# Edge messages of a graph layer on one core: ten routed groups in 28 in place of three in 8, and slot sums after seven of ten routed groups

## The chip, the cores and the metric

The kernel runs on one core of one Trainium2 chip. The metric is device time in microseconds (us): three runs of the kernel before took 2140.23, 2142.25 and 2141.35 us, median 2141.35. The profile is of one more execution, which took 2145.47 us.

## The reference, in short

There are 6250 nodes of 128 numbers and 200,000 edges. Each edge has a source index, a destination index (the edges are sorted by destination), 20 edge features and a weight. All is computed in float32:

```
h    = x @ W_in2f                                      # per node
Wij  = (ssp(f_ij @ W_filt1 + b_filt1) @ W_filt2 + b_filt2) * weight     # per edge
x_ij = h[dst] * Wij                                    # message of an edge
agg  = segment_sum(x_ij, src)                          # added up by source: random order
out  = layernorm(x + ssp(agg @ W_out1 + b_out1) @ W_out2 + b_out2)
```

ssp(v) is softplus(v) - log 2. The gather by destination is over a narrow range of nodes, since the edges are sorted by it. The sum by source is over random nodes, and it is what the change is about.

## The kernel before

**Groups.** Edges are handled in 391 groups of 512 (4 tiles of 128 edges). For each group TensorE computes the filter (first_layer for a pair of groups, second_layer for one), gathers h of the destinations with a one-hot matmul (gather; VectorE's compare_dst makes the one-hot `pick`), ScalarE does the softplus in three passes for each pair (soften_abs, soften_exp, soften_ln) and weighs the gathered rows (weigh_h_dst), VectorE finishes the hidden layer (finish_hidden) and multiplies the message (multiply).

**Two ways to sum by source.** A *plain* group goes to memory: VectorE compares sources (compare_src), TensorE adds up repeated ones inside each tile (sum_repeated), ScalarE copies the totals out of PSUM (copy_total), VectorE makes the indices (mark_repeated, make_index), and GpSimd issues four indirect DMAs that add rows to four tables in HBM (scatter, L778). GpSimd does this for the plain groups in order of their numbers. A *routed* group stays on the chip: ScalarE and VectorE split the message in two parts (split_hi, split_lo), VectorE makes one-hot rows of 896 slots for each of the four tiles (route_one_hot, L1368), TensorE multiplies seven slot tiles of four matmuls each (route, L1726) into unit_psum, and ScalarE copies each tile to a ring in SBUF (keep_slots, L955). A *step* then sums one slot tile number over the newest routed groups: VectorE makes a one-hot of 448 nodes for each (slot_one_hot, L1382, seven buffers), TensorE multiplies (sum_slots, L1746, four matmuls) into unit_psum, and VectorE adds two slices to the accumulator (add_slice, L1397). So each routed group has seven slot tiles to be summed, however many steps there are; a step takes all tiles of its number that lie in the ring.

**Which groups are routed.** Of each period of 8 groups, numbers 1, 4 and 6; after the 48 periods, groups 385 and 388. STEPS_AT says after which routed groups of a period a step is made: after each of the three. TensorE's unit_psum is shared by route and sum_slots, so a step ends only when VectorE has added its slices and the next route begins only when its half is free.

**Order.** Each engine works its instructions in the order in which they are written. For the main stretch this order is written out by hand for one period, in a function `unit(u)` of each engine, and for what is left over in `rest()`. `run_periods` calls unit for every period, unrolled. Every instruction waits on semaphores for what it needs and for its buffer: four buffers each for totals, indices, destination and source loads, two for the one-hot `pick`, and one for route_hot and for moving. SP loads features, dst and src rows and windows in its own written order.

**Last layers.** When all additions have landed, SP loads the four tables (it waits first for the scatter-adds at L710, then for the last slot sum at L711), GpSimd adds them up, and thirteen chunks go through the output layers. The functions that the change touches and their callers follow.

Of the kernel before, what the change touches and what calls it, by code (L numbers as in the profile page):

```python
# [297 lines left out]
def build(nc, t):  # L298
    with ExitStack() as ctx:
# [245 lines left out]
        def _(sp):  # L545
# [114 lines left out]
            def unit(u):  # L660
                def g(n): return plus(u, n)
                def quad(n): return (u[0], u[1] // QUAD + n)
                next_window(g(6))
                next_src(g(7), plain)
                next_dst(g(8))
                next_window(g(7))
                next_dst(g(9))
                next_window(g(8))
                next_src(g(8), plain)
                next_features(quad(6))  # L670
                next_dst(g(10)); next_dst(g(11))
                next_window(g(9)); next_window(g(10))
                next_dst(g(12)); next_dst(g(13))
                next_src(g(10), plain)
                next_window(g(11)); next_window(g(12))
                next_src(g(11), plain)
                next_dst(g(14))
                next_features(quad(7))
                next_src(g(13), plain)
                next_window(g(13))  # L680
                next_dst(g(15))

            def rest():
                next_src((0, 390), plain)
                next_window((0, 390))
# [141 lines left out]
        def _(act):  # L827
# [129 lines left out]
            def unit(u):  # L957
                def g(n): return plus(u, n)
                def pair(n): return (u[0], u[1] // 2 + n)
                def r(n): return (u[0], u[1] // PERIOD * len(ROUTED_AT) + n)  # L960
                copy_total(g(-1), plain)
                soften_abs(pair(2))
                weigh_h_dst(g(2), plain)
                keep_slots(r(-1), 0)
                soften_exp(pair(2))
                copy_total(g(0), plain)
                keep_slots(r(-1), 1); keep_slots(r(-1), 2)
                soften_ln(pair(2))
                keep_slots(r(-1), 3); keep_slots(r(-1), 4); keep_slots(r(-1), 5); keep_slots(r(-1), 6)
                split_hi(r(0))  # L970
                copy_total(g(2), plain)
                weigh_h_dst(g(3), plain)
                soften_abs(pair(3))
                weigh_h_dst(g(4), plain)
                soften_exp(pair(3))
                keep_slots(r(0), 0); keep_slots(r(0), 1)
                soften_ln(pair(3))
                weigh_h_dst(g(5), plain)
                keep_slots(r(0), 2); keep_slots(r(0), 3)
                copy_total(g(3), plain)  # L980
                keep_slots(r(0), 4)
                weigh_h_dst(g(6), plain)
                keep_slots(r(0), 5); keep_slots(r(0), 6)
                soften_abs(pair(4))
                split_hi(r(1))
                soften_exp(pair(4))
                soften_ln(pair(4))
                weigh_h_dst(g(7), plain)
                keep_slots(r(1), 0)
                copy_total(g(5), plain)  # L990
                keep_slots(r(1), 1); keep_slots(r(1), 2)
                weigh_h_dst(g(8), plain)
                soften_abs(pair(5))
                keep_slots(r(1), 3); keep_slots(r(1), 4)
                soften_exp(pair(5))
                soften_ln(pair(5))
                keep_slots(r(1), 5); keep_slots(r(1), 6)
                weigh_h_dst(g(9), plain)
                split_hi(r(2))

            def rest():
                weigh_h_dst((0, 386), plain)
                soften_abs((0, 194))
                keep_slots((0, 143), 0)
                copy_total((0, 383), plain)
                keep_slots((0, 143), 1)
                soften_exp((0, 194))
                keep_slots((0, 143), 2)
                soften_ln((0, 194))
                keep_slots((0, 143), 3)  # L1010
                weigh_h_dst((0, 387), plain)
                keep_slots((0, 143), 4)
                copy_total((0, 384), plain)
                keep_slots((0, 143), 5); keep_slots((0, 143), 6)
                split_hi((0, 144))
                weigh_h_dst((0, 388), plain)
                soften_abs((0, 195))
                soften_exp((0, 195))
                soften_ln((0, 195))
                keep_slots((0, 144), 0)  # L1020
                weigh_h_dst((0, 389), plain)
                keep_slots((0, 144), 1)
                copy_total((0, 386), plain)
                keep_slots((0, 144), 2); keep_slots((0, 144), 3)
                weigh_h_dst((0, 390), plain)
                keep_slots((0, 144), 4)
                copy_total((0, 387), plain)
                keep_slots((0, 144), 5); keep_slots((0, 144), 6)
                split_hi((0, 145))
                keep_slots((0, 145), 0); keep_slots((0, 145), 1)  # L1030
                copy_total((0, 389), plain)
                keep_slots((0, 145), 2); keep_slots((0, 145), 3); keep_slots((0, 145), 4)
                keep_slots((0, 145), 5); keep_slots((0, 145), 6)
                copy_total((0, 390), plain)
# [78 lines left out]
        def _(dve):  # L1113
# [285 lines left out]
            def unit(u):  # L1399
# [13 lines left out]
                slot_one_hot(s(-1), 1)  # L1413
                multiply(g(1), plain)
                slot_one_hot(s(-1), 2)
                compare_src(g(3), plain)
                compare_dst(g(4))
                slot_one_hot(s(-1), 3)
                compare_dst(g(5))
                mark_repeated(g(0), plain)  # L1420
                multiply(g(2), plain)
                slot_one_hot(s(-1), 4)
                make_index(g(0), plain)
                finish_hidden(pair(2))
                slot_one_hot(s(-1), 5)
                route_one_hot(r(0), 0); route_one_hot(r(0), 1)
                slot_one_hot(s(-1), 6)
                route_one_hot(r(0), 2); route_one_hot(r(0), 3)
                split_lo(r(0))
                mark_repeated(g(2), plain)  # L1430
                add_slice(s(-1), 0); add_slice(s(-1), 1)
                make_index(g(2), plain)
                multiply(g(3), plain)
                compare_dst(g(6))
                slot_one_hot(s(0), 0); slot_one_hot(s(0), 1)
                compare_dst(g(7))
                slot_one_hot(s(0), 2); slot_one_hot(s(0), 3)
                multiply(g(4), plain)
                finish_hidden(pair(3))
                slot_one_hot(s(0), 4)  # L1440
                compare_src(g(5), plain)
                compare_dst(g(8))
                slot_one_hot(s(0), 5)
                route_one_hot(r(1), 0); route_one_hot(r(1), 1)
                mark_repeated(g(3), plain)
                slot_one_hot(s(0), 6)
                route_one_hot(r(1), 2)
                slot_one_hot(s(1), 0)
                make_index(g(3), plain)
                multiply(g(5), plain)  # L1450
                slot_one_hot(s(1), 1)
# [493 lines left out]
```

## Time and profile before

| what | value |
|---|---|
| median of three runs | 2141.35 us |
| profiled execution | 2145.47 us |
| its span (first to last instruction) | 2143.7 us |
| TensorE matmul, busy | 2013.4 us |
| VectorE, busy | 1967.4 us |
| ScalarE, busy | 1588.1 us |
| GpSimd, busy | 1664.0 us |
| indirect DMAs of GpSimd | 979 |

Busy time is time in which an instruction of the engine is recorded as running. What lies between two instructions of an engine is idle time, and the profile names what ended it, or says "issue" where it finds nothing that the engine waited for. PE is TensorE, PEld its weight loads, DVE VectorE, ACT ScalarE, POOL GpSimd, and SPq the queue on which SP issues DMAs.

### The profile page before, as it was taken

To read this page: it belongs to the slowest core of one execution; us is meant where nothing else is said; L and a number is where in the kernel's file an instruction comes from. 1 tells how busy PE (TensorE), PEld (TensorE's weight loads), DVE (VectorE), ACT (ScalarE), POOL (GpSimd) and SP (SyncE) were. 2 spreads that over 40 slices of the span, in tenths; PEclk is the share of its full clock that TensorE was granted. 3 is DMA by queue.
4 is the path that set the end of the run, shared out by engine and by line. 5 is a ranking of instruction groups with operands and counts; after the bars stand their busy time and mean duration, and the time that the engine had idled before them with its cause. 6 is when DMAs were issued, how large, how long until landed. Compare 5 with 4: busy or idle time off the path is not lost.

```text
span 2143.7 us, 53463 instructions
## 1 busy us (share of the span) xinstructions
PE 2013.4 (94%) x16433; PEld 1700.4 (79%) x16433; DVE 1967.4 (92%) x4035; ACT 1588.1 (74%) x3852; POOL 1664.0 (78%) x1038
## 2 busy tenths in 40 slices
PE   2589999999999999999999999999999999999946
PEld 2468888888888888888888888888888888888833
DVE  5669999999999999999999999999999999999837
ACT  0278878778788787787877877877878878778517
POOL 2058888888888888888888888888888888888854
PEclk8689999999999999999999999999999999999979
DMA  9546666656666666566666666665666666665574
GB/s 319 212 92 105 102 94 99 104 92 98 102 103 97 100 99 102 90 99 103 95 98 101 100 94 101 99 102 90 99 103 99 96 104 99 102 92 82 89 196 136
DMA packets 346341, 235.28 MB, mean 110 GB/s; under 512 B 86088, under 2 KB 325555, under 8 KB 345851
## 3 DMA queue, kind: packets, MB, share of 16 engines
q0 software_dynamic: 140976, 64.22, 32.6%
q1 hardware_dynamic: 194598, 150.79, 26.9%
q10 hardware_dynamic: 10476, 16.77, 2.1%
q8 instruction: 136, 2.23, 0.4%
q14 instruction: 155, 1.26, 0.2%
HBM read 145.44 MB, written 86.20 MB: 108 GB/s over the span
## 4 chain that ended last, share of the span: by engine, by line
PE 70%; DMA 10%; DVE 8%; issue 6%; POOL 3%; ACT 2%; ACTq 0%; SPq 0%; DVEq 0%; POOLq 0%
PE unit_psum L1726 19%; PE unit_psum L1746 17%; PE both_psum L1682 13%; PE total_psum L1695 8%; DMA table<-total,index 7%; PE pre_psum L1663 7%; PE both_psum L1707 4%; POOL table L778 3%; PE both_psum L1678 2%; DMA src_b<-src 1%; DVE route_hot L1368 1%; DVE scat_hot L1382 1%; DMA b_o<-in_b_o 1%; DVE acc_t L1397 1%; ACT out_rows L1077 1%
## 5 line engine op out<-in xcount | busy, mean ns | idle before, releaser
L778 POOL DMA_INDIRECT table<-total,index x979 | 1605.4, 1640 | 416.6 <-issue 263.9
L1726 PE MATMUL unit_psum<-moving,route_hot 128*128 128x258 f32 x4088 | 637.4, 295 | 2.8 <-DVE acc_t L1397 1.5
L1726 PEld LDWEIGHTS unit_psum<-moving,route_hot 128*128 128x128 f32 x4088 | 526.3, 190 | 48.7 <-ACT ring L955 32.5
L1382 DVE TENSOR_SCALAR scat_hot<-node_iota,ring 128x448 fp32r<-128x448 uint16 x1022 | 473.1, 475 | 17.8 <-PE unit_psum L1746 13.0
L955 ACT ACTIVATE ring<-unit_psum 128x258 fp32r<-128x258 f32 x1022 | 370.3, 402 | 153.0 <-PE unit_psum L1726 139.0
L933 ACT ACTIVATE h_dst<-both_psum,edge_cols 128x128 f32<-128x128 f32 x1564 | 446.1, 379 | 48.8 <-PE both_psum L1707 48.4
L1746 PE MATMUL unit_psum<-scat_hot,ring 64*128 64x448 f32 x4088 | 461.3, 372 | 11.5 <-DVE acc_t L1397 9.7
L1746 PEld LDWEIGHTS unit_psum<-scat_hot,ring 64*128 64x128 f32 x4088 | 378.4, 186 | 87.6 <-ACT ring L955 37.0
L1682 PE MATMUL both_psum<-w_f,hidden 128*128 128x128 f32 x3128 | 422.1, 278 | 0.0
L1368 DVE TENSOR_SCALAR route_hot<-node_iota,slot_cols 128x896 fp32r<-128x896 uint16 x584 | 406.0, 729 | 7.6 <-PE unit_psum L1726 7.0
L1682 PEld LDWEIGHTS both_psum<-w_f,hidden 128*128 128x128 f32 x3128 | 398.5, 192 | 5.5
L896 ACT ACTIVATE soft<-pre_psum 128x1024 f32<-128x1024 f32 x196 | 202.8, 1034 | 101.6 <-PE pre_psum L1663 101.5
L1695 PE MATMUL total_psum<-message,same 128*128 128x129 f32 x1960 | 264.1, 277 | 1.4 <-DVE message L1332 1.4
L1695 PEld LDWEIGHTS total_psum<-message,same 128*128 128x128 f32 x1960 | 240.1, 191 | 4.0 <-DVE message L1332 2.0
L1306 DVE SCALAR_TENSOR_TENSOR hidden<-pre_psum,soft 128x1024 f32<-128x1024 f32 x196 | 237.4, 1211 | 5.6 <-ACT soft L908 5.6
L1663 PE MATMUL pre_psum<-f_t,w_f 32*128 32x512 f32 x784 | 222.8, 644 | 9.0 <-issue 4.0
L915 ACT ACTIVATE total<-total_psum 128x516 f32<-128x516 f32 x245 | 148.7, 607 | 92.7 <-DMA table<-total,index 75.9
L908 ACT ACTIVATE soft<-soft 128x1024 f32<-128x1024 f32 x196 | 212.2, 1083 | 3.1
L902 ACT ACTIVATE soft<-soft 128x1024 f32<-128x1024 f32 x196 | 210.3, 1073 | 0.1
L1397 DVE TENSOR_TENSOR acc_t<-acc_t,unit_psum 128x448 f32<-128x448 f32 x304 | 178.0, 613 | 19.9 <-PE unit_psum L1746 19.1
L1332 DVE TENSOR_TENSOR message<-both_psum,h_dst 128x512 f32<-128x512 f32 x245 | 168.0, 686 | 18.2 <-PE both_psum L1682 14.0
L1707 PEld LDWEIGHTS both_psum<-window,pick 128*128 128x128 bf16 x1564 | 88.7, 98 | 106.5 <-issue 94.3
(124 smaller groups left out, 1561.9 us busy)
## 6 DMA issues: line engine op xcount, KB each, us to landing
dst_b<-dst SPq DMA_DIRECT2D x391, 128.0 KB
src_b<-src SPq DMA_DIRECT2D x245, 128.0 KB
f_t<-in_f_t SPq DMA_DIRECT2D x98, 256.0 KB, 4.1
table<-total,index POOLq DMA_INDIRECT x979
table<-zeros ACTq DMA_DIRECT2D x20, 640.0 KB, 9.9
window<-h_parts SPq DMA_DIRECT2D x391, 32.0 KB
parts<-table SPq DMA_DIRECT2D x48, 256.0 KB, 5.3
h_parts<-h_out SPq DMA_DIRECT2D x12, 384.0 KB, 2.8
```

The source lines that it names most:

```text
L778: pool.indirect_dma_start(tables[k], bass.IndirectOffsetOnAxis(index[:, i, k:k + 1], 0), total[:, i, k, 0:DIM], None, compute_op=ALU.add). ...
L908: act.activation(soft[:, :, :], soft[:, :, :], ACT.Ln, bias=1.0).then_inc(soft_done, 1)
L933: last = act.activation(h_dst[:, b, d], source, ACT.Copy, scale=columns_of(g, kind)[:, weight:weight + 1])
L955: act.activation(ring[:, RING_AT[r[1], k], :], unit_psum[:, k % 2, 0:MOVING], ACT.Copy).then_inc(ring_done, 1)
L1306: dve.scalar_tensor_tensor(hidden[:, first:first + 2, :], pre_psum[:, :, :], 0.0, soft[:, :, :], ALU.max, ALU.add).then_inc(hidden_done, 1)
L1368: hot = dve.tensor_scalar(route_hot[:, tile, :], node_iota[:, :], slot_cols[:, column:column + 1], None, ALU.is_equal)
L1382: dve.tensor_scalar(scat_hot[:, (n - 1) % HOTS, :], node_iota[:, 0:BUCKET], ring[:, RING_AT[r[1], slot_tile(s)], 2 * DIM:2 * DIM + 1].bitc ...
L1663: last = pe.matmul(pre_psum[:, a, :], w_f1[row:row + BAND, :], f_t[row:row + BAND, quad[1] % FEEDS, :], start=True, stop=True)
L1682: last = pe.matmul(filter_psum[:, d], hidden[:, g[1] % QUAD, k * P:(k + 1) * P], w_f2[:, :], start=False, stop=(k == TILES - 1))
L1695: last = pe.matmul(total_psum[:, k // 2, d], same[:, b, k, :], message[:, b, k, :], start=True, stop=True)
L1726: last = pe.matmul(unit_psum[:, k % 2, 0:MOVING], route_hot[:, tile, k * P:(k + 1) * P], moving[:, tile, :], start=(tile == 0), stop=(tile ...
L1746: last = pe.matmul(unit_psum[:, strip, 0:BUCKET], ring[rows, RING_AT[r[1], slot_tile(s)], part * DIM:(part + 1) * DIM], scat_hot[rows, (n ...
```

## The change

The constants of the period change, and with them every written order: SP's, ScalarE's, VectorE's and TensorE's unit and rest. GpSimd's code is the same. No instruction changes its form. The ring, whose size is computed from the constants, has 43 tiles in place of 28.

```diff
-PERIOD = 8
-ROUTED_AT = (1, 4, 6)
-LAST_PERIOD = 384
-LAST_ROUTED = (385, 388)
+PERIOD = 28
+ROUTED_AT = (2, 4, 7, 10, 13, 16, 18, 21, 24, 27)
+LAST_PERIOD = 364
+LAST_ROUTED = (366, 368, 371, 374, 377, 380, 382, 385)
...
-STEPS_AT = (0, 1, 2)
+STEPS_AT = (0, 2, 3, 5, 6, 8, 9)
...
@@ VectorE, unit(u): the first lines of 77 instructions before and of 258 after
-                slot_one_hot(s(-2), 6)
+                route_one_hot(r(-1), 0)
+                slot_one_hot(s(-2), 7)
+                route_one_hot(r(-1), 1)
                 multiply(g(0), plain)
-                split_lo(r(-1))
-                route_one_hot(r(-1), 2); route_one_hot(r(-1), 3)
+                slot_one_hot(s(-2), 8); slot_one_hot(s(-2), 9)
+                route_one_hot(r(-1), 2)
+                mark_repeated(g(-2), plain)
                 slot_one_hot(s(-1), 0)
                 add_slice(s(-2), 0)
-                mark_repeated(g(-1), plain)
-                make_index(g(-1), plain)
+                route_one_hot(r(-1), 3)
+                split_lo(r(-1))
                 add_slice(s(-2), 1)
...
@@ TensorE, unit(u): the first lines
-                sum_slots(s(-2), 1); sum_slots(s(-2), 2); sum_slots(s(-2), 3); sum_slots(s(-2), 4)
-                sum_slots(s(-2), 5); sum_slots(s(-2), 6)
+                route(r(-2), 6)
+                gather(g(2))
+                sum_slots(s(-2), 0); sum_slots(s(-2), 1); sum_slots(s(-2), 2); sum_slots(s(-2), 3)
+                sum_slots(s(-2), 4); sum_slots(s(-2), 5); sum_slots(s(-2), 6); sum_slots(s(-2), 7)
+                sum_slots(s(-2), 8); sum_slots(s(-2), 9)
                 first_layer(pair(2))
-                gather(g(2))
+                gather(g(3))
                 second_layer(g(1))
                 route(r(-1), 0)
...
@@ TensorE, rest(): the end
-                sum_repeated((0, 390), plain)
-                route((0, 145), 5); route((0, 145), 6)
-                sum_slots((0, 145), 0); sum_slots((0, 145), 1); sum_slots((0, 145), 2); sum_slots((0, 145), 3)
...
-                sum_slots((0, 149), 2); sum_slots((0, 150), 0); sum_slots((0, 150), 1); sum_slots((0, 151), 0)
+                sum_repeated((0, 390), plain)
+                sum_slots((0, 100), 0); sum_slots((0, 100), 1); sum_slots((0, 100), 2); sum_slots((0, 100), 3)
+                sum_slots((0, 101), 0); sum_slots((0, 101), 1); sum_slots((0, 102), 0)
```

## Rows read from the trace of the kernel before

**Rows 1.** The page: busy us of each engine, share of the span, instructions.
```profile
PE 2013.4 (94%) x16433; PEld 1700.4 (79%) x16433; DVE 1967.4 (92%) x4035; ACT 1588.1 (74%) x3852; POOL 1664.0 (78%) x1038
```

**Rows 2.** GpSimd in time order, 710 to 752: start us, us, instruction, idle before.
```profile
710.91 1.84 POOL L778 DMA_INDIRECT table<-total,index  x1 [0.30 <-issue]
...
724.53 1.96 POOL L778 DMA_INDIRECT table<-total,index  x1 [0.31 <-issue]
...
742.63 1.54 POOL L778 DMA_INDIRECT table<-total,index  x1 [0.74 <-issue]
744.47 1.54 POOL L778 DMA_INDIRECT table<-total,index  x1 [0.30 <-issue]
746.32 1.54 POOL L778 DMA_INDIRECT table<-total,index  x1 [0.30 <-issue]
```

**Rows 3.** Groups of instructions: busy us, mean ns, idle us before, releasers.
```profile
L778 POOL DMA_INDIRECT table<-total,index x979 | 1605.4, 1640 | 416.6 <-issue 263.9 <-DVE index L1351 107.2 <-DMA table<-total,index 41.3
```

**Rows 4.** VectorE in time order, 710 to 730, columns as in rows 2 (xN: N merged).
```profile
711.03 0.44 DVE L1382 TENSOR_SCALAR scat_hot<-node_iota,ring 128x448 fp32r<-128x448 uint16 x1
711.39 1.27 DVE L1368 TENSOR_SCALAR route_hot<-node_iota,slot_cols 128x896 fp32r<-128x896 uint16 x2
...
725.73 0.67 DVE L1368 TENSOR_SCALAR route_hot<-node_iota,slot_cols 128x896 fp32r<-128x896 uint16 x1
```

**Rows 5.** Single tiles: ns min/median/max, first and last start us.
```profile
L1382 DVE TENSOR_SCALAR scat_hot<-node_iota,ring x1022: 431/444/781, 140.1 to 2046.7; 128x448 fp32r<-128x448 uint16 x171
L1368 DVE TENSOR_SCALAR route_hot<-node_iota,slot_cols x584: 666/679/1024, 129.1 to 2019.8; 128x896 fp32r<-128x896 uint16 x195
L1296 DVE TENSOR_SCALAR pick<-dst_b,edge_cols x391: 333/345/683, 108.3 to 2012.7; 128x512 bf16<-128x512 uint16 x196
L1342 DVE TENSOR_SCALAR moved<-total,order_twice,spare_row x245: 270/279/606, 126.6 to 2031.3; 128x4 f32<-128x4 f32 x123
L1286 DVE TENSOR_TENSOR same<-src_b,edge_cols x245: 671/679/695, 113.7 to 2013.2; 128x512 f32<-128x512 uint16 x123
L1397 DVE TENSOR_TENSOR acc_t<-acc_t,unit_psum x304: 600/614/624, 142.9 to 2055.8; 128x448 f32<-128x448 f32 x152
```

**Rows 6.** Stretches: us, then busy us of PE, PEld, DVE, ACT, POOL, clock, DMA.
```profile
128.90:2046.50 1917.60, 1903.58 (x15909) 1624.45 (x15909) 1840.25 (x3744) 1510.20 (x3687) 1605.40 (x979) 1.00 0.62 99
2046.50:2143.70 97.20, 53.16 (x242) 30.83 (x238) 52.56 (x160) 47.77 (x114) 46.64 (x39) 0.82 0.62 167
```

**Rows 7.** Groups as in rows 3: TensorE's matmuls of the two kinds.
```profile
L1726 PE MATMUL unit_psum<-moving,route_hot 128*128 128x258 f32 x4088 | 637.4, 295 | 2.8 <-DVE acc_t L1397 1.5 <-ACT ring L955 0.3
L1746 PE MATMUL unit_psum<-scat_hot,ring 64*128 64x448 f32 x4088 | 461.3, 372 | 11.5 <-DVE acc_t L1397 9.7 <-ACT ring L955 0.9 <-DVE scat_hot L1382 0.9
L1695 PE MATMUL total_psum<-message,same 128*128 128x129 f32 x1960 | 264.1, 277 | 1.4 <-DVE message L1332 1.4
```

**Rows 8.** Groups as in rows 3: VectorE and ScalarE.
```profile
L1382 DVE TENSOR_SCALAR scat_hot<-node_iota,ring 128x448 fp32r<-128x448 uint16 x1022 | 473.1, 475 | 17.8 <-PE unit_psum L1746 13.0 <-ACT ring L955 2.3
L1397 DVE TENSOR_TENSOR acc_t<-acc_t,unit_psum 128x448 f32<-128x448 f32 x304 | 178.0, 613 | 19.9 <-PE unit_psum L1746 19.1
L1368 DVE TENSOR_SCALAR route_hot<-node_iota,slot_cols 128x896 fp32r<-128x896 uint16 x584 | 406.0, 729 | 7.6 <-PE unit_psum L1726 7.0
L955 ACT ACTIVATE ring<-unit_psum 128x258 fp32r<-128x258 f32 x1022 | 370.3, 402 | 153.0 <-PE unit_psum L1726 139.0
```

**Rows 9.** What SP's queue waited for: us in total, times, longest.
```profile
SPq L623 <- PE both_psum L1707: 513.4, 161, 6.3
SPq L590 <- DVE pick L1296: 479.2, 236, 8.1
...
SPq L711 <- PE unit_psum L1746: 7.1, 1, 7.1
```

**Rows 10.** TensorE in time order, 2048 to 2060.
```profile
2050.97 1.86 PE L1746 MATMUL unit_psum<-scat_hot,ring 64*128 64x448 f32 x8 [1.24 <-DVE acc_t L1397]
2054.08 1.11 PE L1746 MATMUL unit_psum<-scat_hot,ring 64*128 64x448 f32 x4 [1.25 <-DVE acc_t L1397]
```

More of the change, by code:

```diff
@@ L1431, in unit @@
+                mark_repeated(g(1), plain)
+                make_index(g(1), plain)
+                slot_one_hot(s(-1), 9)
+                compare_src(g(5), plain)
                 add_slice(s(-1), 0); add_slice(s(-1), 1)
[L1432 to L1435, printed above, removed]
+                slot_one_hot(s(0), 0)
+                multiply(g(4), plain)
+                slot_one_hot(s(0), 1); slot_one_hot(s(0), 2)
@@ L1462, in unit @@
+                route_one_hot(r(2), 1); route_one_hot(r(2), 2)
+                split_lo(r(2))
+                route_one_hot(r(2), 3)
+                slot_one_hot(s(1), 2)
+                multiply(g(9), plain)
+                slot_one_hot(s(1), 3)
+                mark_repeated(g(6), plain)
+                compare_dst(g(12))
+                make_index(g(6), plain)
+                finish_hidden(pair(6))
+                multiply(g(10), plain)
+                compare_src(g(11), plain)
                 slot_one_hot(s(1), 4)
-                make_index(g(5), plain)
@@ new lines, in unit @@
+                slot_one_hot(s(2), 6)
+                mark_repeated(g(11), plain)
+                slot_one_hot(s(2), 7); slot_one_hot(s(2), 8)
+                finish_hidden(pair(8))
+                slot_one_hot(s(2), 9)
+                compare_dst(g(17))
+                multiply(g(14), plain)
+                split_lo(r(4))
+                make_index(g(11), plain)
+                add_slice(s(2), 0); add_slice(s(2), 1)
+                compare_src(g(15), plain)
+                multiply(g(15), plain)
@@ new lines, in unit @@
+                compare_dst(g(25))
+                slot_one_hot(s(4), 5); slot_one_hot(s(4), 6)
+                route_one_hot(r(7), 0)
+                multiply(g(23), plain)
+                mark_repeated(g(19), plain)
+                split_lo(r(7))
+                compare_dst(g(26))
+                route_one_hot(r(7), 1)
+                make_index(g(19), plain)
+                compare_src(g(25), plain)
+                route_one_hot(r(7), 2)
+                slot_one_hot(s(4), 7)
+                multiply(g(24), plain)
@@ new lines, in unit @@
+                compare_dst(g(28))
+                mark_repeated(g(22), plain)
+                make_index(g(22), plain)
+                route_one_hot(r(8), 0); route_one_hot(r(8), 1); route_one_hot(r(8), 2)
+                split_lo(r(8))
+                route_one_hot(r(8), 3)
+                multiply(g(26), plain)
+                finish_hidden(pair(14))
+                mark_repeated(g(23), plain)
+                compare_dst(g(29))
+                compare_src(g(29), plain)
+                slot_one_hot(s(5), 2); slot_one_hot(s(5), 3)
@@ new lines, in unit @@
+                route(r(4), 1); route(r(4), 2)
+                second_layer(g(16))
+                route(r(4), 3); route(r(4), 4)
+                gather(g(17))
+                route(r(4), 5); route(r(4), 6)
+                sum_repeated(g(14), plain)
+                first_layer(pair(10))
+                gather(g(18))
+                second_layer(g(17))
+                sum_repeated(g(15), plain)
+                route(r(5), 0); route(r(5), 1)
+                second_layer(g(18))
+                route(r(5), 2); route(r(5), 3)
@@ new lines, in unit @@
+                first_layer(pair(12))
+                gather(g(22))
+                route(r(6), 0); route(r(6), 1)
+                second_layer(g(21))
+                route(r(6), 2)
+                sum_repeated(g(19), plain)
+                route(r(6), 3)
+                second_layer(g(22))
+                route(r(6), 4)
+                gather(g(23))
+                route(r(6), 5); route(r(6), 6)
+                first_layer(pair(13))
+                gather(g(24))
+                second_layer(g(23))
```

1103 lines of the change are left out of this document (907 added, 196 removed).

## Prediction

> **What bounds the kernel now.** I read the page's busy shares first. They point at TensorE (94%) and VectorE (92%), and show GpSimd at 78% [rows 1]. The next view is GpSimd's own instructions in time order over one period of eight groups [rows 2]. Each scatter-add starts 0.30 us after the previous one ended, whatever that one took; the reader is to see that the column "idle before" hardly ever rises above 0.30 and is put down to "issue". The shortest scatter-adds last 1.54 us, so the floor of one is 1.54 + 0.30 = 1.844 us from start to start (742.63 to 744.47 to 746.32 shows it). The grouped row [rows 3] gives the whole: 979 of them, mean 1.640 us, 416.6 us idle before them, of which 104.5 us lie before the first. That is 1605.4 + 312.1 = 1917.5 us, from 128.9 to 2046.5 us, which is the whole main stretch. GpSimd is never without work there. It is 78% "busy" and 100% occupied, because the 0.30 us between two scatter-adds is not counted. So the main stretch is 979 x 1.959 us, and of the 1.959 us, 1.844 is floor and 0.115 is waiting.
>
> What is the 0.115? The smaller part is a gap now and then (the 0.74 us before 742.63). The larger, 0.098 us each, is scatter-adds that last longer than 1.54 us. Their long forms stand where VectorE runs one-hot comparisons: the scatter-add at 710.91 took 1.84 us and the one at 724.53 took 1.96 us, while VectorE ran route_hot from 711.39 to 712.66 and from 725.73 [rows 2, 4]. The comparisons are slowed in return: all four kinds of tensor_scalar have a long tail (route_hot 666 to 1024 ns, scat_hot 431 to 781, pick 333 to 683, moved 270 to 606), and the tensor_tensor kinds have none (same 671 to 695, acc_t 600 to 624) [rows 5]. Two parties that stretch each other, and only in one kind of instruction, share something.
>
> TensorE is close behind: 1903.6 us busy of the 1917.6 [rows 6]. VectorE has 1840.3.
>
> **The change, part by part.** Counted from the constants: before there are 48 periods x 3 + 2 = 146 routed and 245 plain groups; after, 13 x 10 + 8 = 138 routed and 253 plain. Steps of slot sums fall from 152 to 103, each taking ten groups' slots instead of seven in the steady part; slot tiles fall from 1022 to 966.
>
> *TensorE.* A routed group costs (637.4 + 461.3) / 146 = 7.53 us in the route and slot-sum matmuls, a plain one 264.1 / 245 = 1.08 us [rows 7]. Eight groups moved: 8 x (7.53 - 1.08) = -51.6 us.
>
> *VectorE.* 56 scat_hot at 0.463 (-25.9), 32 route_hot at 0.695 (-22.2), 8 split_lo at 0.68, the length of the tensor_tensor `same` of equal size [rows 5] (-5.4), 98 slice adds at 0.586 (-57.4); plus 8 x (0.68 + 0.28) = +7.7 for compare_src and mark. Sum -103 us [rows 5, 8]. *ScalarE:* 56 ring copies at 0.362, -20 us [rows 8]; the copies of totals and of moving nearly cancel.
>
> None of these three is worth anything by itself while GpSimd sets the pace: 1903.6 - 51.6 = 1852 us of TensorE lies below even the floor of GpSimd after the change.
>
> *GpSimd.* 8 plain groups more are 32 scatter-adds more, 1011. At the pitch of before this costs 32 x 1.959 = +62.7 us. The floor rises from 1805 to 1011 x 1.844 = 1864.3 us. This is the term that no cover hides.
>
> *The waits of the scatter-adds* are the unknown. Nothing in the trace shows the new orders, so I bound them. Upper end: 0.115 us each, as now: 1980.5 us. Lower end: none at all: 1864.3 us. What is between them: the comparisons' time for each scatter-add, by medians of [rows 5], is now (1022 x 0.444 + 584 x 0.679 + 391 x 0.345 + 245 x 0.279) / 979 = 1.076 us and becomes (966, 552, 391 and 253 of the same) / 1011 = 0.998 us, 7% less. The orders themselves can be counted too: a comparison in a run takes its median less the 0.08 by which neighbours overlap (711.03 to 711.39 for one of 0.44 us [rows 4]), so 0.36 for scat_hot, 0.60 for route_hot, 0.26 for pick and 0.20 for moved. The time by which runs of comparisons, with no other instruction between them, exceed 0.95 us is then 7.4 us in the old unit, 0.37 for each of its 20 scatter-adds, and 18.3 us in the new one, 0.25 for each of 72: ten of twelve route_one_hot stand in pairs before, about half of forty afterwards. (The 0.95 is half of the floor of 1.844, an estimate of what fits once the scatter-add must get in twice; it serves to compare the orders and no more.) Scaled with the first the stretch of 0.098 becomes 0.091, with the second 0.067. I take the second and 0.010 for gaps, 0.077 in all, because VectorE also gets a real reserve (103 us) in which its comparisons can be late without anyone waiting. Pitch 1.921, stretch 1942.1 us.
>
> The Trainium skill (SBUF - State Buffer, "Who interferes with whom") says that a VectorE instruction in a 2-port mode and a GpSimd instruction exclude each other for the whole length, and that tensor_scalar may enter that mode where tensor_tensor may not. The second half agrees with the tails above. The first half does not hold here as it stands: 1.076 us of comparisons and 1.54 us of scatter-add cannot lie one behind the other in 1.959 us.
>
> *Queues.* SP issues 8 more src loads of 128 KB and places all its loads in the new order; it waits for VectorE and TensorE for nearly 1000 us of the span in the two longest entries [rows 9], so its loads are early. Cost 0, or 1 us per load that comes late. The scatter's order on GpSimd is unchanged: group by group.
>
> *Start.* The first scatter-add waits for the first total; group 0 is plain in both. The routing tables of 584 columns shrink to 552 ahead of it: -1.5 to 0, taken as 0. It stays at 128.9.
>
> *End.* Now the last landed scatter-add is not the last event: SP's wait on the tables ends, and then it waits 7.1 us more for the last slot sum [rows 9], because after the last total TensorE still has 28 slot tiles in seven short steps, each handed over by VectorE's adds (1.24 and 1.25 us idle before the last two [rows 10]). After the change only 7 tiles in 3 steps stand behind the last sum_repeated, while the last five groups (386 to 390) are all plain and give GpSimd 19 scatter-adds in a row. So GpSimd ends last and the 7.1 us go: the tail of 97.2 us [rows 6] becomes 90.1. Bounds 97.2 and 90.1; what is late next is GpSimd itself.
>
> *Sum.* 128.9 + 1942.1 + 90.1 = 2161 us of span, against 128.9 + 1917.6 + 97.2 = 2143.7. The profiled execution took 2145.5, 1.8 above its span, and the median of the runs is 2141.35, 4.1 below that. So take 2.3 off: **2159 us**, 0.8% slower. With bounds of the wait: 2081 (none) to 2197 (as now). Equality is at a pitch of (2143.7 - 219.0) / 1011 = 1.904 us, a wait of 0.060 us: the change gains only if it halves what the scatter-adds wait.
>
> **Rivals.**
>
> *A. The waits do not fall.* Comparisons still meet a scatter-add as often as they do now. 0.095 to 0.115 us each gives 2179 to 2197. For it: the comparisons' time falls by 7% only, and a phase between two engines over 72 scatter-adds is harder to hold than over 20. Against: VectorE's reserve.
>
> *B. Faster: each microsecond of comparison that is taken away gives its whole length back.* Place: the main stretch. Price: 1.076 - 0.998 = 0.078 us for each scatter-add, so the wait falls to 0.037 and the pitch to 1.881: 1901.7 + 219.0 = 2121, **2118 us**. It decides from a wait of 0.060 down. For it: TensorE is 99% busy now, so GpSimd's waits of before may have been in the shadow of a TensorE that had no more to give, and with 52 us less there they are free to shrink; three large ones of a period (0.30 and 0.42 of length, and the gap's 0.44 above 0.30 [rows 2]) are 1.2 of its 20 x 0.115 = 2.3 us, and an order that avoids those alone stands at 0.055. Against: the many small ones remain. (The Trainium skill's lock for the whole length, in the section named above, is the reading by which all the time taken away comes back.)
>
> *C. The engines are bound by TensorE as before and GpSimd keeps up.* Then the 51.6 us of TensorE would show in full: 2141 - 52 = 2090. Against: GpSimd's floor alone gives 2081, and it would need waits of 0.009. I give it the low end of B only.
>
> *D. A new wait.* A step sums ten slot tiles, and there are seven scat_hot buffers, so TensorE can hold unit_psum half way while VectorE writes three more; the route matmuls and ring copies queue behind. 1 us in each of 103 steps, if GpSimd runs dry by it: 2159 + 50 at most. Against: TensorE has some 90 us of reserve below 1942.
>
> **How the numbers follow.** Two runs of this kernel can be told apart from about 0.2%, 4.3 us, a wait of 0.004 us up or down: "the same" is a wait of 0.056 to 0.064. Chances: forecast (0.064 to 0.095) 0.34; A 0.17; D 0.03; the same 0.08; B with C 0.38. So faster 0.38, same 0.08, slower 0.54. The range leaves out the waits under 0.03 and over 0.114: 2112 to 2196. The likeliest case by itself is 2146 to 2178.
>
> **What would show it.** GpSimd: 1011 scatter-adds, gaps of 0.30 throughout, mean length near 1.60 us; under A 1.63 and more, under B 1.57. The first at 128.9 and the last near 2069. TensorE less busy in the main stretch than its 99% now, VectorE near 90%. SP's wait for the slot sum gone. If GpSimd's idle time in front of scatter-adds grows beyond 0.32 us each with "DVE index" or "ACT total" as releaser, the bound has moved and the argument is wrong; if the mean length is below 1.58 us, only the size of the wait was.

## The result, and the profile after

The changed kernel takes **2227.26 us** (median of four runs, 2219.77 to 2230.95) against 2141.52 us for the kernel before beside it. The ratio is 1.0398, 95% interval 1.0377 to 1.0418: 4% slower. The forecast of 2159 us had the direction right; the size was wrong, and the time lies above the range of 2112 to 2196.

The page of the changed kernel, busy us of each engine, with the granted clock in 40 slices. It answers to [rows 1].

```profile
PE 2018.5 (91%) x16049; PEld 1677.4 (76%) x16049; DVE 1879.1 (85%) x3865; ACT 1575.2 (71%) x3788; POOL 1721.6 (78%) x1070
...
PEclk8589999999999999999999999999999999999969
...
L860 POOL DMA_INDIRECT table<-total,index x1011 | 1663.0, 1645 | 443.8 <-issue 278.7
```

The shares of PE and DVE fell and GpSimd's stayed at 78%. The last line answers to [rows 3]: 1011 scatter-adds as counted, mean 1.645 us (1.640 before). The two stretches that answer to [rows 6], then three short ones; columns as there (us, busy us of PE, PEld, DVE, ACT, POOL, clock, DMA share, GB/s):

```profile
127.30:2129.30 2002.00, 1911.44 (x15547) 1603.45 (x15545) 1756.36 (x3580) 1495.17 (x3617) 1662.97 (x1011) 0.98 0.61 96
2129.30:2217.80 88.50, 47.92 (x212) 27.93 (x212) 47.89 (x150) 47.72 (x114) 46.66 (x39) 0.83 0.70 183
427.80:434.60 6.80, 6.80 (x30) 5.07 (x30) 4.62 (x10) 3.78 (x11) 5.89 (x4) 0.50 0.43 52
571.20:578.00 6.80, 6.60 (x27) 4.87 (x28) 5.28 (x11) 3.69 (x11) 5.69 (x4) 0.50 0.49 59
578.00:694.00 116.00, 111.44 (x925) 93.70 (x924) 103.44 (x212) 89.92 (x216) 95.12 (x59) 1.00 0.59 93
```

The main stretch is 2002.0 us, 1011 x 1.980. The two short stretches show something that the main stretch of before did not have until its last few steps: TensorE at a granted clock of 0.50, that is 1.2 GHz, while it is busy. Read through in consecutive stretches of a few us, there are twelve such places up to 2107 us, five of some 6.8 us and seven of some 3.4, 58 us in all. In the kernel before there is none between 125 and 2033 us.

The terms of the prediction's own sum, in us. The floor is 1.54 us of scatter-add and 0.304 us to the next one:

| term | predicted | measured | before |
|---|---|---|---|
| start, to the first scatter-add | 128.9 | 127.3 | 128.9 |
| floor, 1.844 each | 1864.3 | 1864.3 | 1805.3 |
| scatter-adds longer than 1.54 | 67.7 | 106.1 | 97.7 |
| gaps above 0.304 | 10.1 | 31.7 | 14.6 |
| tail | 90.1 | 88.5 | 97.2 |
| span | 2161.1 | 2217.8 | 2143.7 |
| median less span | -2.1 | +9.5 | -2.3 |

(Measured: 1663.0 - 1011 x 1.54 = 106.1, and 2002.0 - 1663.0 - 1011 x 0.304 = 31.7.) Two terms failed, both inside "the waits of the scatter-adds": 60 us of the miss of 68. These waits, the stretch and the gaps together, are 0.136 us each, not 0.077. Start and tail take 3 back, and the other runs of the changed kernel lie 6 to 11 us above the profiled one, so that its median is 9.5 above the span.

**Where the gaps come from.** Before, [rows 2], the idle time in front of a scatter-add was 0.30 us almost always. GpSimd of the changed kernel, in time order:

```profile
595.84 2.09 POOL L860 DMA_INDIRECT table<-total,index  x1 [0.30 <-issue]
599.38 1.55 POOL L860 DMA_INDIRECT table<-total,index  x1 [1.45 <-issue]
...
605.41 1.59 POOL L860 DMA_INDIRECT table<-total,index  x1 [0.30 <-issue]
609.37 1.91 POOL L860 DMA_INDIRECT table<-total,index  x1 [2.37 <-issue]
```

The profile says "issue", but VectorE made the index of the scatter-add at 599.38 only at 598.37:

```profile
597.77 0.68 DVE L1571 TENSOR_TENSOR same<-src_b,edge_cols 128x512 f32<-128x512 uint16 x1
598.37 0.15 DVE L1636 TENSOR_TENSOR index<-moved,edge_cols 128x4 int32<-128x4 f32 x1
```

GpSimd runs dry there. Of such gaps 20 are over 0.6 us; from 462 us on they come one to three times in each period of some 143 us. Ahead of them, ScalarE and TensorE in time order:

```profile
566.40 0.40 ACT L1037 ACTIVATE ring<-unit_psum 128x258 fp32r<-128x258 f32 x1
570.47 0.60 ACT L997 ACTIVATE total<-total_psum 128x516 f32<-128x516 f32 x1 [3.67 <-DMA table<-total,index]
570.97 0.66 ACT L1037 ACTIVATE ring<-unit_psum 128x258 fp32r<-128x258 f32 x2
```

```profile
566.48 1.22 PE L2306 MATMUL unit_psum<-moving,route_hot 128*128 128x258 f32 x8
567.54 0.40 PE L2287 MATMUL both_psum<-window,pick 128*128 128x128 bf16 x4
571.40 2.09 PE L2306 MATMUL unit_psum<-moving,route_hot 128*128 128x258 f32 x8 [3.46 <-ACT ring L1037]
```

ScalarE's copy of the totals (L997) waits 3.67 us until the scatter-adds that read the same one of the four buffers have landed. The ring copy stands behind it in ScalarE's order, and the route matmuls wait for the ring copy, so TensorE idles 3.46 us. After that the same eight matmuls take 2.09 us in place of 1.22: the clock has been halved. A second way leads over VectorE. At 691.46 the copy of the totals waited 4.04 us; VectorE's mark of repeated rows waits for that copy, a comparison stands behind the mark, and TensorE waits for the comparison:

```profile
692.09 0.29 DVE L1627 TENSOR_SCALAR moved<-total,order_twice,spare_row 128x4 f32<-128x4 f32 x1 [2.61 <-ACT total L997]
692.50 0.67 DVE L1667 TENSOR_SCALAR scat_hot<-node_iota,ring 128x448 fp32r<-128x448 uint16 x1
693.22 0.67 PE L2326 MATMUL unit_psum<-scat_hot,ring 64*128 64x448 f32 x4 [2.77 <-DVE scat_hot L1667]
```

ScalarE's waits for landings, in all, times, and longest, of the changed kernel and of before:

```profile
ACT total L997 <- DMA table<-total,index: 140.4, 56, 11.6
```

```profile
ACT total L915 <- DMA table<-total,index: 75.9, 62, 3.3
```

Of the 140.4, 17.7 lie in two waits of the last plain groups (2098.82 and 2108.62); the others above 2.5 us come about once a period or twice, as at 385, 530, 675, 816 and 960, and at 427, 570 and 691. Of the 20 large gaps of GpSimd 16 follow an idle time of TensorE of 1.98 us or more, by 26 to 56 us. A fall of the clock is not needed for it: one of 0.93 us at 1175.6 follows an idle time of 2.11, and one of 2.18 at 1475.3 an idle time of 2.77, and after both the granted clock stayed at 1.00:

```profile
1141.92 1.22 PE L2306 MATMUL unit_psum<-moving,route_hot 128*128 128x258 f32 x8 [2.11 <-ACT ring L1037]
...
1428.84 1.22 PE L2306 MATMUL unit_psum<-moving,route_hot 128*128 128x258 f32 x8 [2.77 <-ACT ring L1037]
```

That the idle times bring the gaps about is read from this order of events; experiment 4 tests it.

### The profile page after: what moved, and what is told of

It is laid out like the page before. It is cut to its first block and busy times, and to the rows that moved or that the text cites. A ratio compares the mean times of both kernels' runs of the same rounds, so it can differ in the third digit from the quotient of the medians.

```text
span 2217.8 us, 52283 instructions
## 1 busy us (share of the span) xinstructions
PE 2018.5 (91%) x16049; PEld 1677.4 (76%) x16049; DVE 1879.1 (85%) x3865; ACT 1575.2 (71%) x3788; POOL 1721.6 (78%) x1070
## 3 DMA queue, kind: packets, MB, share of 16 engines
q8 instruction: 133, 2.18, 0.4%
## 5 line engine op out<-in xcount | busy, mean ns | idle before, releaser
L860 POOL DMA_INDIRECT table<-total,index x1011 | 1663.0, 1645 | 443.8 <-issue 278.7
L2306 PE MATMUL unit_psum<-moving,route_hot 128*128 128x258 f32 x3864 | 615.0, 297 | 34.9 <-ACT ring L1037 28.9
L2306 PEld LDWEIGHTS unit_psum<-moving,route_hot 128*128 128x128 f32 x3864 | 503.7, 191 | 94.2 <-ACT ring L1037 43.7
L1667 DVE TENSOR_SCALAR scat_hot<-node_iota,ring 128x448 fp32r<-128x448 uint16 x966 | 446.5, 483 | 17.8 <-PE unit_psum L2326 16.5
L2326 PE MATMUL unit_psum<-scat_hot,ring 64*128 64x448 f32 x3864 | 441.4, 373 | 19.5 <-DVE scat_hot L1667 8.6
L1653 DVE TENSOR_SCALAR route_hot<-node_iota,slot_cols 128x896 fp32r<-128x896 uint16 x552 | 381.0, 712 | 44.4 <-PE unit_psum L2306 43.9
L2326 PEld LDWEIGHTS unit_psum<-scat_hot,ring 64*128 64x128 f32 x3864 | 350.8, 185 | 75.7 <-DVE scat_hot L1667 17.1
L2275 PE MATMUL total_psum<-message,same 128*128 128x129 f32 x2024 | 280.3, 282 | 7.5 <-ACT total L997 7.5
L997 ACT ACTIVATE total<-total_psum 128x516 f32<-128x516 f32 x253 | 154.2, 609 | 172.9 <-DMA table<-total,index 140.4
L2275 PEld LDWEIGHTS total_psum<-message,same 128*128 128x128 f32 x2024 | 255.5, 197 | 11.3 <-issue 9.3
L2243 PE MATMUL pre_psum<-f_t,w_f 32*128 32x512 f32 x784 | 229.4, 661 | 10.1 <-issue 4.0
L2287 PEld LDWEIGHTS both_psum<-window,pick 128*128 128x128 bf16 x1564 | 97.7, 99 | 134.0 <-issue 119.6
L1571 DVE TENSOR_TENSOR same<-src_b,edge_cols 128x512 f32<-128x512 uint16 x253 | 171.1, 682 | 3.2 <-DMA h_parts<-h_out 2.2
```

The source lines that it names most:

```text
L860: pool.indirect_dma_start(tables[k], bass.IndirectOffsetOnAxis(index[:, i, k:k + 1], 0), total[:, i, k, 0:DIM], None, compute_op=ALU.add). ...
L1653: hot = dve.tensor_scalar(route_hot[:, tile, :], node_iota[:, :], slot_cols[:, column:column + 1], None, ALU.is_equal)
L1667: dve.tensor_scalar(scat_hot[:, (n - 1) % HOTS, :], node_iota[:, 0:BUCKET], ring[:, RING_AT[r[1], slot_tile(s)], 2 * DIM:2 * DIM + 1].bitc ...
L2243: last = pe.matmul(pre_psum[:, a, :], w_f1[row:row + BAND, :], f_t[row:row + BAND, quad[1] % FEEDS, :], start=True, stop=True)
L2275: last = pe.matmul(total_psum[:, k // 2, d], same[:, b, k, :], message[:, b, k, :], start=True, stop=True)
L2306: last = pe.matmul(unit_psum[:, k % 2, 0:MOVING], route_hot[:, tile, k * P:(k + 1) * P], moving[:, tile, :], start=(tile == 0), stop=(tile ...
```

## The experiments

The letters in the expectations stand for the theories as they are told there. A pair has the same edit in both kernels. Times are medians; ratios are to the kernel before, run beside them (2142.39, 2142.56 and 2143.91 us).

**1. Is GpSimd the bound of either kernel?** The question is what 32 scatter-adds are worth: they are left out in both, the fourth tile of every seventh plain group up to the 224th (the sums for those tiles are then missing).

```diff
+def left_out(n, k):
+    return k == 3 and n % 7 == 0 and n <= 224
...
                 for k in range(tiles_in(g)):
+                    if kind is plain and left_out(through(g, kind), k):
+                        continue
```

> The changed kernel with 32 scatter-adds left out (the fourth one of every seventh plain group), so it has 979 as the kernel before. Theory P (GpSimd paces the main stretch, each scatter-add costs its pitch of 1.98 us): 2227 - 63 = about 2164 us. Rival T (the written orders pace it, and GpSimd is only full because the others hand it work at that rate): at most a third of that, 2205 to 2227.

> The kernel before with 32 scatter-adds left out in the same way, 947 remain. P: 32 x 1.959 = -63, about 2079 us. Rival Q (TensorE, 99% busy in the main stretch, is the bound too): TensorE's idle time there is 14 us, so no more than -14, 2127 to 2141.

Measured: changed kernel with 979 left 2169.24 us, 1.0127 (1.0103 to 1.0151), 58.0 us less than with 1011, or 1.81 us for each. Before with 947 left 2138.25 us, 0.9977 (0.9968 to 0.9987): 4 us, where the prediction's reading would give 32 x 1.959 = 63. Its row, columns as [rows 3]:

```profile
L789 POOL DMA_INDIRECT table<-total,index x947 | 1555.4, 1642 | 462.5 <-issue 288.6 <-DVE index L1362 123.8 <-DMA table<-total,index 43.7
```

Fewer scatter-adds, and more idle time before them (462.5 against 416.6). So the changed kernel, with 1011, is bound by GpSimd and the kernel before was not: it was at the point where GpSimd just keeps up. The page of before had a sign of this that the prediction did not use, the chain of work that ended last:

```profile
PE 70%; DMA 10%; DVE 8%; issue 6%; POOL 3%; ACT 2%; ACTq 0%; SPq 0%; DVEq 0%; POOLq 0%
```

At an equal number, 979, the new order is 27 us slower than the old. Its trace has 43.0 us of gaps above the floor, where the kernel before has 14.6 and the same stretch to within 2 us; why the new order leaves GpSimd dry so often even then was not found. The changed kernel's time at halved clock falls with those 32, from 58 us to 14 ahead of its last stretch, and to 7 with the 759 of experiment 2 and none without scatter-adds: it depends on them.

**2. Three of four scatter-adds** (the fourth tile's are left out everywhere).

```diff
+    return k == 3
```

> The changed kernel with three scatter-adds for a plain group in place of four (the fourth is left out in all; 758 remain). GpSimd has 758 x 1.84 = 1400 us of work, so it can't be the bound. What is left is the order's own time on TensorE, VectorE and ScalarE. P: below the same edit of the kernel before, since TensorE has 52 us and VectorE 103 us less: about 2080. T: the order itself is slow and stays above 2150.

> The kernel before with three scatter-adds for a plain group in place of four (734 remain). P and Q: TensorE becomes the bound, 1903.6 us of the 1917.6: about 2128, hardly faster. If it falls by more than 30 us, then much of TensorE's recorded busy time was waiting too, and TensorE's 99% said little.

Measured: changed kernel (759 left) 2134.35 us, 0.9955 (0.9941 to 0.9969); before (735 left) 2129.84 us, 0.9944 (0.9927 to 0.9962). With GpSimd a quarter relieved, both kernels stand at nearly the same time, and the changed one has no lead. It came out between its two theories (2080, and over 2150), and the kernel before at the 2128 expected. From 979 scatter-adds to 759 the changed kernel gains only 35 us, 0.16 for each: GpSimd has then stopped being what holds it.

**3. No scatter-adds at all**, what the order of the other engines alone can do.

```diff
+    return True
```

> The changed kernel with no scatter-adds at all: the written orders alone, and VectorE without anyone at its port. If the order's own waits made 2134 us of the run with three scatter-adds (theory O), it stays at 2120 to 2134. If it was VectorE, slowed by scatter-adds (theory V), it falls to TensorE's work: 2141 - 52 = about 2090.

> The kernel before with no scatter-adds at all. Q (TensorE bounds): 2120 to 2130, as with three for a group. V: VectorE, 96% busy with some 90 us of stretching in it, falls back and releases TensorE: below 2110.

Measured: changed kernel 2109.19 us, 0.9849 (0.9832 to 0.9865); before 2127.81 us, 0.9934 (0.9918 to 0.9951). So scatter-adds cost the kernel before some 15 us in all, and the changed one 118 us. The changed kernel again lies between its theories (2120 or more, and 2090). The new order by itself wins 19 us, not the 52 that its TensorE work was counted at. The 1400 us in the middle of the kernel before, without scatter-adds:

```profile
400.00:1800.00 1400.00, 1400.00 (x11783) 1200.14 (x11783) 1309.68 (x2766) 1117.12 (x2731) 0.00 (x0) 1.00 0.24 66
```

TensorE has no recorded idle moment there. The ends of matmuls are modelled in the profile, so that alone would not make it the bound; but the number of its matmuls in those 1400 us is the same whatever is taken from the other engines: 11784 with 735 scatter-adds, 11783 with none, and 11800 with the shorter comparisons of experiment 5, against 11714 in the kernel before. So TensorE's rate bounds the kernel before, as far as these runs go: ScalarE, 80% busy, was relieved in none of them. The comparisons show what they and the scatter-adds do to each other. First the changed kernel with its scatter-adds, then without (ns min/median/max, first and last start):

```profile
L1667 DVE TENSOR_SCALAR scat_hot<-node_iota,ring x966: 432/447/802, 140.6 to 2108.6; 128x448 fp32r<-128x448 uint16 x194
L1653 DVE TENSOR_SCALAR route_hot<-node_iota,slot_cols x552: 666/681/1020, 126.3 to 2075.5; 128x896 fp32r<-128x896 uint16 x184
```

```profile
L1678 DVE TENSOR_SCALAR scat_hot<-node_iota,ring x966: 439/447/456, 139.5 to 2012.6; 128x448 fp32r<-128x448 uint16 x194
L1664 DVE TENSOR_SCALAR route_hot<-node_iota,slot_cols x552: 674/681/689, 125.4 to 1982.7; 128x896 fp32r<-128x896 uint16 x184
```

The tail of [rows 5] is gone (802 to 456, 1020 to 689): the comparisons were stretched by scatter-adds and by nothing else.

**4. Six buffers in place of four** for totals, moved rows and indices. It takes away much of what the copy of the totals waits for. (`same`, the result of compare_src, moves to the old place of the totals.)

```diff
-        moved = sb("moved", [P, QUAD, TILES], F32)
-        index = sb("index", [P, QUAD, TILES], I32)
+        moved = sb("moved", [P, 6, TILES], F32)
+        index = sb("index", [P, 6, TILES], I32)
+        total = sb("total", [P, 6, TILES, ROW], F32)
...
-            g0 = last_before(g, kind, QUAD)
+            g0 = last_before(g, kind, 6)
```

> The changed kernel with six buffers in place of four for a plain group's totals, moved marks and indices (all three indexed by the group's number modulo 6; `same` takes the old place of `total`). Theory S (ScalarE's total copy waits for landed scatter-adds, up to 5 us in a period and 140 us in all; everything behind it on ScalarE waits, TensorE runs empty, and its clock is halved for 58 us of the main stretch): the waits fall below 70 us, the halved stretches become few, and the time falls by 25 to 50 us, to 2177 to 2202. Rival P (GpSimd's own work and port waits alone): GpSimd's pitch is what it is, at most -8, 2219 or more.

> The kernel before with six buffers in the same way: control. It has no halved clock in its main stretch and 76 us of such waits, none over 3.3 us; TensorE bounds it. Both theories: within 5 us of 2142.

Measured: changed kernel 2192.19 us, 1.0234 (1.0215 to 1.0254), 35.1 us less; before 2139.88 us, 0.999 (0.998 to 0.9999). The changed kernel's rows, the group and ScalarE's wait:

```profile
L861 POOL DMA_INDIRECT table<-total,index x1011 | 1656.0, 1638 | 421.2 <-issue 248.1 <-DVE index L1637 108.3 <-DMA table<-total,index 60.0
```

```profile
ACT total L998 <- DMA table<-total,index: 74.2, 46, 4.6
```

The wait for landings halves (140.4 to 74.2), the gaps fall from 31.7 to 10.2 us, the stretch from 106.1 to 99.1, the pitch from 1.980 to 1.952; of the 58 us at halved clock some 37 are left, in eight places. The time lies where theory S has it (2177 to 2202), with waits a little above its 70, and P (2219 or more) is refuted. The gaps are now what the prediction took (10.1). The stretch is not. In the kernel before the same edit takes the waits for landings from 75.9 to 4.1 us and the time by 0.1%: waits of ScalarE that hardly held anyone up.

**5. Are the scatter-adds stretched in proportion to the comparisons?** The comparison of route_hot is made over 448 of its 896 columns from the second routed group on (the other half keeps its first values), some 0.233 us less for each of about 550, with six buffers in the changed kernel and four in the one before.

```diff
-                hot = dve.tensor_scalar(route_hot[:, tile, :], node_iota[:, :], ...
+                w = SLOT_ROWS if r[1] == 0 else 448
+                hot = dve.tensor_scalar(route_hot[:, tile, 0:w], node_iota[:, 0:w], ...
```

> The changed kernel with six buffers, and from the second routed group on route_hot is compared over 448 of its 896 columns (the other half keeps old values): 551 x 4 comparisons' length halves, some 0.31 us each, 170 us less of VectorE time at the shared port, 0.17 us for each scatter-add out of 1.00. Theory W (a scatter-add's wait shrinks in proportion): 0.098 becomes 0.081, -17 us, about 2175. Rival B (time taken away at the port comes back whole): the wait goes to zero, 1011 x 1.844 + 219 = 2083, held up by the order at 2109. Nothing at all would say that it is not the port.

> The kernel before with the same halved comparison. Q (TensorE bounds, GpSimd costs 14 us on top): 2128 to 2138. If VectorE or the port had been the bound there, 2110 or less.

Measured: changed kernel 2172.46 us, 1.0135 (1.0118 to 1.0152), 19.7 us less than with six buffers alone; before 2133.17 us, 0.9946 (0.9929 to 0.9963). The row of the changed one:

```profile
L861 POOL DMA_INDIRECT table<-total,index x1011 | 1640.7, 1623 | 418.6 <-issue 247.7 <-DVE index L1637 109.4 <-DMA table<-total,index 56.5
```

About 550 x 0.233 = 128 us of comparison were taken away; 15.3 us came back in the length of the scatter-adds (1656.0 to 1640.7) and 3.5 in the gaps. W, the theory of a proportion, is near: its 17 us were worked out for 170 us of comparison, and for 128 of the 1009 us it gives 12.6 where the length shows 15.3. That the whole length comes back (rival B) is off by a factor of six. In the kernel before, 11 us come back, and TensorE is then at the full rate of experiment 3.

**6. Why is the new order only 19 us faster without scatter-adds?** Two suspects, each taken away from the changed kernel without scatter-adds: too few scat_hot buffers for a step of ten tiles (rival D), and the second buffer of h_dst.

```diff
-HOTS = 7
+HOTS = 10
```

```diff
-        h_dst = before_x(20512, "h_dst", [P, 2, GROUP], F32)
+        h_dst = at(44384, "h_dst", [P, 3, GROUP], F32)
```

> The changed orders alone (no scatter-adds) with ten scat_hot buffers in place of seven. They take 2109 us where TensorE's smaller work would allow 2090. Rival D of the prediction (a step of ten tiles runs out of seven buffers): -10 to -19. Theory O (the waits lie elsewhere in the written orders): within 5 us of 2109.

> The changed orders alone with three buffers for the weighed rows (h_dst) in place of two. ScalarE waits 85 us there for VectorE's message of two groups before, and 0.3 us in the kernel before. Theory H (this wait holds ScalarE, the ring copies behind it and so TensorE): -10 to -19. Otherwise within 5 us of 2109.

Measured: 2110.42 and 2110.11 us, ratios 0.9846 and 0.9843, against 2109.19 without either edit. Neither does anything to the time here, without scatter-adds; with them neither was tried. What can be read is on TensorE's weight loads without scatter-adds, changed kernel and before (busy, mean ns, idle us before them, releasers):

```profile
L2317 PEld LDWEIGHTS unit_psum<-moving,route_hot 128*128 128x128 f32 x3864 | 499.6, 190 | 59.1 <-issue 34.3 <-ACT ring L1048 12.4 <-DVE moving L1654 11.9
L2273 PEld LDWEIGHTS both_psum<-w_f,hidden 128*128 128x128 f32 x3128 | 399.3, 193 | 17.0 <-issue 11.1
L2337 PEld LDWEIGHTS unit_psum<-scat_hot,ring 64*128 64x128 f32 x3864 | 350.8, 184 | 62.5 <-DVE acc_t L1693 7.2 <-ACT ring L1048 6.5 <-DVE scat_hot L1678 6.4
```

```profile
L1737 PEld LDWEIGHTS unit_psum<-moving,route_hot 128*128 128x128 f32 x4088 | 526.2, 190 | 41.8 <-ACT ring L966 36.8 <-issue 1.2 <-DVE moving L1369 0.6
L1693 PEld LDWEIGHTS both_psum<-w_f,hidden 128*128 128x128 f32 x3128 | 398.6, 193 | 5.5
L1757 PEld LDWEIGHTS unit_psum<-scat_hot,ring 64*128 64x128 f32 x4088 | 376.3, 185 | 86.1 <-ACT ring L966 37.8 <-DVE acc_t L1408 11.2 <-DVE scat_hot L1393 0.8
```

All weight loads together are 1697.9 us busy before and 1655.3 after, 42.6 less. Idle time in front of the slot sums falls by 23.6 us (86.1 to 62.5), as fewer steps should give; in front of route it rises by 17.3, of the second layer by 11.5, and of the gather by 11.3 (107.0 to 118.3), most of it without a releaser. The span less the busy time of weight loads rises from 428.6 to 451.8 us, 23 more, and 42.6 less 23 is the 19 us measured. It must come out so, since busy and idle time make up the span; it says where the time is, not what causes it.

## Why the prediction was wrong, step by step

**What bounds the kernel before: wrong.** "So the main stretch is 979 x 1.959 us" is true as a description, and no cause. That GpSimd is never without work [rows 2, 3] was taken for "GpSimd sets the pace"; 32 fewer scatter-adds gave 4 us and not 63, and none at all gave 15. TensorE, 99% busy in [rows 6] and called "close behind", was the bound. The two stood within 1% of each other, so GpSimd's waits of 0.115 us were in part slack: it took the time that TensorE left it. Rivals B and C named this possibility, and drew from it that the waits would shrink and the time fall.

**32 more scatter-adds cost 62.7 us: nearly right, as it turned out**, since the change makes GpSimd the bound: the last 32 cost 58.0.

**The waits, 0.077 each: the step that failed**, 60 us of the miss. It has two parts.
The stretch, taken as 0.067, is 0.105 in the changed kernel, 0.098 with six buffers, and was 0.0998 before (the prediction has 0.098). The count of runs of comparisons that exceed 0.95 us, 0.37 to 0.25 for each scatter-add, predicted a fall by a third that did not come; the plain time of comparison for each scatter-add (7% less, giving 0.091) would have been nearer, and experiment 5 shows a dependence of that kind, weak: 0.127 us less comparison for each scatter-add, 0.015 us less stretch. Why the order of the comparisons counted for nothing stays open. Rival A had "the waits do not fall", with a chance of 0.17; that is right of the stretch, but its 2179 to 2197 has no gaps beyond those of before, and the time lies 30 us above it. Where the Trainium skill (SBUF - State Buffer, "Who interferes with whom") has the later of the two instructions blocked for the whole of the other, the runs agree that tensor_scalar is party to it (the tails of experiment 3) and not on the price: 128 us of comparison taken away gave back 19.7.

The gaps, taken as 0.010, are 0.031. No step of the prediction held what makes them. It asked what new wait could stop TensorE and looked at scat_hot (rival D; ten buffers did nothing without scatter-adds, and the wait of 2.77 us for scat_hot before 693.22 comes from the totals and not from a lack of buffers; TensorE's weight loads wait 17.1 us for it in all, 1.5 before, and what part of that is D was not tested). It did not ask what a GpSimd that runs late does to those ahead of it: the four buffers of totals are freed by landed scatter-adds, ScalarE waits for them with the ring copies behind, and VectorE's mark with comparisons behind, TensorE idles and in most cases then runs at half its clock, and, in the period shown, 26 and 36 us later GpSimd runs dry. Six buffers take 35.1 us off. With them the rest of the sum holds: the measured pitch of 1.952, a wait of 0.108, put into it gives 1973.5 + 219.0 - 2.1 = 2190 us, and 2192.19 were measured. That tests start and tail, not the wait. What the two extra buffers are worth is shown; how much of it is the clock and how much the idle time itself was not separated.

**TensorE -51.6 us, "worth nothing by itself": right in the verdict, wrong in the size.** Without scatter-adds the order gives 19 us. The 51.6 was built from the busy time of groups of matmuls, and these overlap: the groups of the kernel before without scatter-adds sum to about 2419 us while TensorE is busy for 2004.0. By what undisturbed matmuls take from the first to the next group's first (route 0.131 us each, slot sums 0.102, repeated sums 0.100) it is 224 x 0.233 - 64 x 0.100 = 46 us, and by the means of the whole kernel (0.135, 0.109 and 0.111) 48. So the overlap is the small part of the error; the rest went into the idle time of experiment 6, whose cause stays open.

**Start, tail, queues: right.** 127.3 and 88.5 us against 128.9 and 90.1. SP's last wait ahead of the tables is now for the scatter-adds alone, and the one for the slot sum [rows 9] is gone:

```profile
SPq L596 <- DVE same L1571: 519.6, 98, 13.5
SPq L590 <- DVE pick L1581: 510.7, 137, 10.5
...
SPq L792 <- DMA table<-total,index: 34.3, 1, 34.3
```

VectorE is busy for 1756.4 of 2002.0 us, 88% where "near 90%" stood, and TensorE for 95% in place of 99%. The sign that the prediction gave for its own failure, idle time beyond 0.32 us for each scatter-add, is there (339.0 / 1011 = 0.335), though not under the names of "DVE index" or "ACT total": the profile puts most of it down to "issue".

**After all, where the 86 us are:** 62.7 for the 32 scatter-adds at the old pitch, 21.6 for the pitch, of 1.980 where it was 1.959 (some 17 of it in the gaps, the rest in the stretch), -10.3 for start and tail, and +12 for medians that lie otherwise to the profiled runs. The new order's gain is nowhere in this, since TensorE is no longer what ends last. Of the kernels that do all the work the fastest is the one before with six buffers (2139.88 us, 0.999), a gain at the edge of what can be told.

## What to carry to other kernels

An engine that always has its next instruction waiting need not be the bound; read the chain that ended last, leave a few per cent of its work out and see whether the time follows (here 4 us of 63), because the price of work moved to it depends on that. Where work is moved onto an engine that is nearly full, follow the buffers that it frees late: who waits for them, and what stands behind that wait in the same written order; two more buffers were worth 35 us here and under 3 in the kernel that was not late. Prices of matmuls are taken from start to start, not from busy times that overlap; and even a right price (46 to 48 us here) is not the gain (19 us) until the order lets it through.

## What was not expected of the hardware

TensorE's granted clock fell to 0.50 in the middle of an otherwise steady stretch, after single idle times such as the 3.46 us before 571.40, and stayed there for 6.8 us of full work (571.20 to 578.00) before it was back at 1.00. Eight route matmuls then take 2.09 us, not 1.22, so one wait of ScalarE costs TensorE about twice its length there: an estimate of 3.46 us idle and some 3.4 more, since 27 matmuls stand in those 6.8 us and 54 in as long a part of the 116 us at 1.00 behind them. The idle time alone does not tell whether the clock falls: after 2.77 us before 1428.84 it stayed at 1.00, and after 1.98 us before 1570.89 it was at 0.50 for 6.8 us. The comparisons and the scatter-adds stretch each other (comparisons from 456 up to 802 ns), but weakly on the whole: each microsecond of comparison taken away gave 0.15 us back.
